# Order of the transfers on SyncE's queue in a fused attention and expert kernel: the first half of the stack ahead of the reciprocals, the second half behind them

## The reference

```
h = concat(tokenise(x), txt)                     # per image 1024 + 32 = 1056 tokens of 64 channels
qkv = layernorm(h) @ w_qkv.T                     # 4 heads of 16 channels
attn = softmax(q @ k.T / 4)
h = h + (attn @ v) @ w_proj.T + b_proj
h = h + sum over the 2 best of 8 experts of gate * (gelu(layernorm(h) @ W1 + b1) @ W2 + b2)
```

## Time and profile before

| | us |
|---|---|
| median of 3 runs | 956.65 |
| lowest and highest | 951.9, 962.88 |
| the profiled execution | 950.68 |
| its span in the trace | 948.9 |

### The profile page before, as it was taken

The page is one execution under the profiler, slowest core; times in us unless marked ns, Lnnn a source line. Parts: engine busy times, 40 slices in busy tenths (PEclk is TensorE's granted clock), DMA queues, the critical chain, the costliest instruction groups (busy, mean ns, idle before and its releaser), DMA issues. The chain is left out here.

```text
span 948.9 us, 15011 instructions
## 1 busy us (share of the span) xinstructions
PE 827.7 (87%) x5664; PEld 328.0 (35%) x5664; DVE 552.6 (58%) x1193; ACT 462.9 (49%) x1061; POOL 131.8 (14%) x148
## 2 busy tenths in 40 slices
PE   5674899987997998799799879979998679999995
PEld 5240232342342234234223423423334134445442
DVE  5033754576876457687645767767783227565642
ACT  0010254554664455466445556646665335565653
POOL 0010100011101001110100111010010025454564
PEclk9975579998998999899999999999999579999998
DMA  8409470109436100843610060061000072918280
GB/s 149 69 34 150 86 82 1 35 3 129 88 57 83 45 1 3 120 87 67 82 47 1 2 82 1 3 82 47 3 13 2 16 166 44 183 43 168 66 167 24
DMA packets 62049, 60.03 MB, mean 63 GB/s; under 512 B 23953, under 2 KB 54297, under 8 KB 61977
## 3 DMA queue, kind: packets, MB, share of 16 engines
q1 hardware_dynamic: 61977, 59.07, 35.4%
HBM read 38.83 MB, written 2.57 MB: 44 GB/s over the span
## 5 line engine op out<-in xcount | busy, mean ns | idle before, releaser
L903 DVE TENSOR_REDUCE max_parts<-bank 128x1 f32<-128x512 f32 x512 | 331.6, 684 | 177.2 <-PE bank L1070 175.1
L825 ACT ACTIVATE probs<-bank 128x384 f32<-128x384 f32 (+1 forms) x768 | 312.4, 465 | 196.0 <-PE bank L1033 194.9
L1033 PE MATMUL bank<-q_stack,k_stack 99*128 99x384 bf16 (+1 forms) x768 | 230.6, 329 | 4.2 <-ACT probs L825 3.8
L1070 PE MATMUL bank<-k_stack,q_stack 96*128 96x512 bf16 x512 | 207.4, 408 | 15.9 <-DMA k_stack<-part 13.1
L1011 PE MATMUL bank<-probs,v_tiles 128*32 128x384 f32 (+1 forms) x1536 | 159.7, 489 | 1.7 <-ACT heads_out L810 1.6
L1033 PEld LDWEIGHTS bank<-q_stack,k_stack 99*128 99x128 bf16 x768 | 72.9, 100 | 205.6 <-ACT probs L825 154.2
L1244 ACT ACTIVATE hid<-bank,biases 128x704 f32<-128x704 f32 x96 | 77.6, 844 | 56.0 <-PE bank L1304 55.8
L1273 DVE SCALAR_TENSOR_TENSOR prod<-bank,biases,cwb 128x352 f32<-128x352 f32 x96 | 55.4, 580 | 60.6 <-PE bank L1289 56.0
L1231 POOL TENSOR_TENSOR acc<-acc,prod 128x352 f32<-128x352 f32 x84 | 78.2, 932 | 59.7 <-DVE prod L1273 55.7
L784 POOL TENSOR_TENSOR part<-qk_rest,part 128x352 bf16<-128x352 f32 x24 | 20.4, 852 | 422.0 <-DVE part L951 422.0
L1047 PE MATMUL bank<-x,tok_m 128*64 128x512 f32 x256 | 69.0, 637 | 8.0 <-DMA text_in<-in_txt 8.0
(11 more groups left out here) (146 smaller groups left out, 612.7 us busy)
## 6 DMA issues: line engine op xcount, KB each, us to landing
cwb<-gates_by_expert SPq DMA_DIRECT2D x24, 704.0 KB, 12.7
x<-in_x SPq DMA_DIRECT2D x64, 256.0 KB, 9.1
q_stack<-part SPq DMA_DIRECT2D x48, 132.0 KB, 5.9
k_stack<-part SPq DMA_DIRECT2D x48, 132.0 KB, 6.4
h_res<-h_new SPq DMA_DIRECT2D x4, 528.0 KB, 3.0
recip<-recip_rows SPq DMA_DIRECT2D x32, 66.0 KB, 2.5
h_all<-h_res SPq DMA_DIRECT2D x4, 528.0 KB, 3.0
out<-outs SPq DMA_DIRECT2D x16, 128.0 KB, 2.4
```

The costliest lines, as they stand in the source:

```text
L825: nc.scalar.activation(probs[:, group % 3, h, 0:n], src, ACT.Exp, scale=SCALE).then_inc(exp_done, 1)
L903: nc.vector.tensor_reduce(max_parts[:, c, H * j + h, i % 2:i % 2 + 1], src[:, :], AX.X, ALU.max)\
L1033: last = nc.tensor.matmul(bank[:, 0:n], ks[par][0:ROWS + 3, h, P * kt:P * kt + P], qs[par][0:ROWS + 3, h, QC[qc]], start=True, stop=True)
L1070: last = nc.tensor.matmul(bank[:, :], queries(h, j), ks[par][0:ROWS, h, HALF * (i % 2):HALF * (i % 2) + HALF], start=True, stop=True)
```

## The change

Two things change in the lists. `spread` had all its three steps at unit 0, and has them now at units 0, 2 and 2 (`AT_SPREAD`). `stack` stood at units 3 and 12, and stands now at units 1 and 3; in slot 0, where 4 units are added to each, at 5 and 7 where it was 7 and 16.

```
--- before.py
+++ after.py
@@ -54,7 +54,8 @@
 AT_RECIP = 8
 AT_NORMALISE = [24, 26, 28]
 AT_FINISH = [27, 30, 33]
-AT_STACK = [3, 12]
+AT_SPREAD = [0, 2, 2]
+AT_STACK = [1, 3]
 AT_EMBED = [list(range(34, 49, 2)), list(range(50, 65, 2))]
 AT_VARY = [74, 75, 76]
 AT_ROOT = [77, 78, 79, 80]
@@ -282,8 +283,8 @@
 
             ahead = q + 1 if par else q + 2
             order = []
-            if u == 0 and "finish" in stages:
-                for i in range(3):
+            for i in range(3):
+                if "finish" in stages and u == AT_SPREAD[i]:
                     order.append(("spread", i, b - 1, 1 - par, q, g))
             for i in range(2):
                 if "following" in stages and u == AT_STACK[i] + (AT_FIRST["project"][-1] if "first" in stages else 0):
```

## The result

| | before | changed |
|---|---|---|
| median, us | 956.99 (4 runs) | 914.35 (4 runs) |
| lowest, highest | 951.9, 962.88 | 909.25, 925.37 |
| the profiled execution | 950.68 | 910.11 |
| its span | 948.9 | 908.3 |
| PE busy | 827.7 (87%) | 813.8 (90%) |

The ratio is 0.9535, with a 95% interval of 0.9439 to 0.963. In a second comparison of the same two kernels, with 6 and 11 runs, it is 0.9584 (0.9498 to 0.967), so the two comparisons put the gain at 4.2 and 4.7%. PE is busy for 14 us less with the same matmuls: before, more of them ran at the lower clock.

What follows compares the result with a forecast made beforehand. PE (busy 87%) bounds the kernel, with its largest wait for chunk 1's shift. 29.1 + 14.4 - 2.0 = 41.5 us gives 909.2 for the profiled execution, 915 on the median; own range 908 to 921, 8 in 10 907 to 930.

Steps and rivals of the forecast that it cites:

- The backlog: Slots 1 to 6: PE's wait for chunk 1's shift, behind twelve stack transfers at about 115 GB/s, goes: 29.1 us.
- The reciprocals: Behind the first six transfers they land at 215.6, 1.2 us later (bounds 0 and 2.0); PE's cover 2.1 us.
- The residual: Wait for chunk 1's shift left in slots 1 to 6: 0.3 us each, 2 us in all.
- The long count: First stack issue to PE's release, 16.97 us, less 7.05 for six transfers: the shift lands at 227.4.
- Rival 3: In slots without the wait another takes its place, in DVE's maxima or `m_part`: 945 to 957 us, chance 0.03.
- the prediction's own sign: Wrong if L1146 waits for POOL, the shift takes over 5 us, or PE's idling returns elsewhere in the slot.
- The clock: After the wait in slots 1 to 6 PE runs at a lower clock; mean 2.4 us a slot, 14.4 us regained.
- What I put outside: Slot 0 (bounds 0.3 us either way), slot 7 without a stack, and phase 2 were to stay as they were.
- Rival 1: The wait shrinks to about 2 us in each slot, clock holding; costs 12 us, 925 on the median, chance 0.12.
- Rival 2: The 9.2 us landing is the shift's own; only 0.9 us gained in six slots, 951 on the median, chance 0.05.
- Rival 4: Reciprocals held behind the first half make PE wait at L1146; 1.1 us more a slot, 7 us slower, chance 0.03.
- The second rule: Each DMA engine consumes descriptors in ring order, so the 16.5 KB reciprocals stand behind 0.8 MB; spoke against the change.

Runs made afterwards that it cites:

- the sweep: Changed kernel with 2, 4, 8, 10 or 12 of the 12 stack transfers ahead of the reciprocals: 937.91, 916.13, 915.79, 938.94, 951.16 us.
- the profile of the table's third column: Changed kernel with slot 0's stack back at its old units (7 and 16), in the five-round comparison: 918.8 us, ratio 0.9634 to the kernel before.
- The two further profiles: Changed kernel with slot 0's stack at its old units, first run (909.74 us), and the changed kernel's second profile (five rounds: 913.26 us, 0.9584).

## Why the prediction was right, step by step

**The time.** 915 was forecast and 914.35 measured, on the median; on the profiled executions 909.2 forecast and 910.11 measured. The mechanism was right, but so close a number is partly luck: the six slots gained 38.1 us where 41.5 were forecast, and 3.0 us came from slot 7, where nothing was changed. The 3.4 us are what is left of four differences: the clock gave back 4.3 less, a new wait for DVE took 2.7, the remaining wait was 1.8 shorter, and other waits of PE shrank by 1.7.

**The backlog (29.1 us).** Right in mechanism and size. The count of 7.05 us for six transfers came out as 7.05 in the run with all twelve ahead, and the sweep has the expected slope on both sides. The trace had shown it: the same DMAs took 3.4 us in slot 0 and 9.2 in slot 1. The fixed and variable cost of a transfer in the Trainium skill ("DMA: Bandwidth & Descriptors", "Anatomy of one DMA") would have had no backlog at all. That section gives it for transfers issued from GpSimd, which the prediction did not say, and the stack is issued from SP. The rows decide, 14.1 us for twelve against 3.7.

**The reciprocals.** Landing forecast at 2.7 us behind the issue, with 3.5 as the bound; 3.2 measured in slot 1, 3.1 to 3.2 in four others, and 4.3, outside the bound, in slot 4. POOL 1.2 us later (219.63 and 218.42, in slots that begin 0.5 us apart, so 1.7). No wait at L1147, as said. The chosen 1.2 us of delay was 0.5 short of the 1.7. What the prediction did not see is that the later POOL meets DVE's steps for the maxima (the next two points).

**The residual (2.0 us).** Mis-sized at its own line, 0.18 us, and larger elsewhere. The long count itself was good: 16.97 us from the first stack issue behind the reciprocals to PE's release, less 1.175 for each transfer fewer, gives 14.62 with 2 ahead and 12.27 with 4 ahead, and the timelines of slot 1 have 14.59 (232.31 - 217.72) and 12.25 (227.25 - 215.00). With 6 ahead the count gives 227.25, and PE came only at 228.26, because it had first waited 1.07 us at L1093.

**Rival 3** (another wait takes the place of this one, in DVE's maxima or `m_part`) had "nothing" for it and came true in small: the waits for DVE at unit 26 in slots 1 to 6 went from 1.1 to 3.8 us. By the prediction's own sign ("if PE's idling comes back at another line within the same slot") it was wrong for these 2.7 us. It had named `m_part` as the next thing late; it is the part just before it.

**The clock (14.4 us).** Slots 1 to 6 as one stretch, with the same matmuls: before, in the changed kernel, and in the profile of the table's third column:

```profile
205.37:680.01 474.64, 431.74 (x3007) 152.04 (x3006) 319.13 (x648) 263.21 (x673) 29.32 (x34) 0.96 0.32 51
...
204.84:641.37 436.53, 421.61 (x3008) 151.24 (x3008) 321.56 (x648) 263.44 (x673) 29.21 (x34) 0.99 0.33 56
...
206.80:641.84 435.04, 416.87 (x3009) 150.15 (x3008) 322.54 (x648) 263.22 (x673) 29.28 (x34) 1.00 0.33 56
```

PE is busy for 10.1 and 14.9 us less. Where the clock stayed up through all six slots, the third line, the term is 14.9, so the excess behind the six waits had been read rightly from the rows. In the changed kernel's first profile the clock fell at three other places, which had no such falls before (341 to 345, 494 to 499 and 597 to 601 us, the last behind a wait of 1.12 us for DVE), and 10.1 are left. The two further profiles have 10.6 and 7.7. So the term is right for what the waits cost, and too large by 3.6 us on the average of the four profiles, because the clock then fell elsewhere, which the prediction had at nothing.

**What I put outside.** Slots 0 and 7 and phase 2 were to stay. Slot 0 changed by -0.9 us (98.52 to 97.58), slot 7 by -3.0 (86.23 to 83.25) and phase 2 by +1.0. Of slot 7's the clock's falls are the likely cause, since its instructions are the same: before, the clock was at the lower level for 14 us at 736 to 750, and the changed kernel has 5 us at 685 to 690. That is inferred from the stretches, not tested. In the thirteen profiles in which slot 7 has the same instructions it takes 81.93 to 86.23 us, and the kernel before has the longest. So the 3.0 us are no gain of the change.

**Rival 1** had a price of 12 us for waits of 2 us in six slots, with the clock holding. The price was wrong: with 2 transfers ahead the waits are 13.9 us more than with 4 (15.1 against 1.2), and the time, in the same runs, 21.8 us more (937.91 against 916.13). The clock fell behind all six, where the prediction had it hold. **Rival 2** fell with the stack behind the shift. **Rival 4** holds as a mechanism and was placed right: with twelve ahead PE waits 5.26 us at L1147 in slot 1, where the prediction had 5.1 for as long an occupation, and the gain is gone. The time is level with before (0.9977) and not 7 us slower. One of its figures is wrong by its own sum: a landing at 224 us costs 1.1 + 1.4 us a slot, 15 us and 966, and not 19 us and 970.

**The second rule** of the Trainium skill, that each DMA engine consumes descriptors in ring order (same page, "Queues, rings and completion order"), agrees with the trace as far as one queue goes (3.2 us behind six transfers, 7.5 behind twelve). But it is not what holds the shift: on POOL's queue it was as late. The prediction didn't need the difference; the run that moved the shift to POOL's queue, with POOL's multiplications and the loads of `x` moved too, lost 1.4%.

## What to carry to other kernels

When an engine waits for a small DMA, compare its issue-to-landing time with the same DMA elsewhere in the trace: 9.2 us against 3.4 pointed at the bytes ahead of it as the cause, and the runs bore it out. Then look for idle time of the queue ahead of the large transfers, and move as many of them there as the next small transfer in line can bear; count bytes over the measured rate on both sides, and expect a floor between the two waits. A second queue did not shorten this backlog, and waits of 2 to 3 us cost PE more than their length (13.9 us of waits, 21.8 us of time). Moving transfers also moves what waits for them: look at what the later engine now runs beside.

## What was not expected of the hardware

- A 3 KB DMA on POOL's queue landed 9.0 us (median) after its issue while SP's queue had the stack and `x` under way, as late as on SP's queue; in slot 7 of the same run, with the DMA engines almost idle, it landed in 1.7 us.
- The granted clock fell to the lower level (1.2 GHz) behind each of PE's waits of 2.17 to 9.55 us in slots 0 to 6 (leaving out the one at 107 us, where it was low already), in some cases only when PE was busy again. Behind waits of 1.1 to 1.8 us it fell in some cases (behind 1.35 us with 8 ahead) and not in others (1.49 us in the second profile of that kernel); behind 1.98 us (slot 0 with 4 ahead) it did not. It also fell where PE had not been idle for over 0.5 us in the 10 us ahead, at 341 to 345 us in the changed kernel.
- After the wait of 13.1 us near the start, the clock came back between 119 and 122 us or between 129 and 131, in executions of one and the same kernel too (119 and 131 with slot 0 as before; 120 and 130 with 8 ahead). Slot 0's later wait depends on which.
- Two small DVE operations that take 0.17 us otherwise took 0.83 and 0.65 us while POOL's multiplication was under way (slot 1 of the changed kernel).
